# A resampling kernel on one core: the results and the bilinear pass are read from PSUM bank by bank, bank 0 by ScalarE and bank 1 by VectorE

## The chip, the cores and the metric

The kernel runs on one core of one Trainium2 chip. The metric is the device time of one execution in microseconds (us), the median of the runs.

## The reference, cut to what matters

Two layers follow each other on an input of 8 x 512 x 128 x 128 fp32. The first makes a half-size image by a grouped convolution, clusters its channels, fits a mixture to get gates, and adds a gated bilinear enlargement to its input. The second adds a bias, enlarges by 2 with a 12-tap filter along both axes, bends the values (leaky ReLU), and reduces by 2 with the filter again.

```python
def _forward(sx, w_down, w_conv, w_up):
    x = conv(sx, w_down, stride 2, groups)            # 8 x 256 x 64 x 64
    ...                                               # clusters, mixture -> gate
    pre_up = gate[:, :, None, None] * x + x
    up = jnp.repeat(pre_up, 2, axis=1) * w_up[None, :, None, None]
    return _bilinear_up_x2(up) + sx                   # 8 x 512 x 128 x 128

def _L1_conv_ref(input, bias, up_filter, down_filter):
    out = input + bias[None, :, None, None]
    out = _sep_upfirdn(out, up_filter * 2, 2, 1, UP_PAD)     # 256 x 256 a channel
    out = jax.nn.leaky_relu(out, 0.2) * 2.0 ** 0.5
    return _sep_upfirdn(out, down_filter, 1, 2, DOWN_PAD)    # 128 x 128 a channel
```

## The kernel before, in words

The convolutions, clusters and mixture fill the first 1.5 ms. The rest, some 5.9 ms, is `resample()`, and the change lies in it alone. It works on 4096 channel images (8 x 512) in 1024 **units** of four. All filters are matrices that TensorE multiplies with, in quadrants of 64 x 64. A unit goes through these steps, software-pipelined over several slots:

- SP loads the image tile `img` (256 KB), and for every second unit the half-size tile `low` (two loads of 16 rows of channels each).
- The **bilinear pass**: TensorE multiplies `low` with `lin` along the rows (L1217, `b1_acc`, in columns 256 to 383 of banks 0 and 1), ScalarE copies both halves to `low_v` (L1273), and GpSimd (POOL) widens it along the other axis in `widen`, the **lift**: `low_d` (L1050), a small copy (L1051), `low_f` (L1053), `lift` (L1056). POOL also adds the bias to `img` (L1041).
- VectorE makes `x_sum` = lift x coef + img in four instructions of 128 elements (L1315).
- **first_up** (TensorE into banks 0 and 1, `u1_acc`), copied to `up1`, half by ScalarE (L1260), half by VectorE (L1300). **second_up** (banks 2 to 5, `u2_acc`).
- The bend, twice two instructions: ScalarE writes 0.2 of the value to `slope_t` (L1251), VectorE takes the maximum into `leaky` (L1291). "Bend 0" and "bend 1" are the pairs for e = 0 and 1.
- **first_down** (banks 6 and 7, `d1_acc`), copied to `dn` by ScalarE (L1282, `d1_out`). **second_down** (banks 0 and 1, columns 0 to 255, `d2_acc`), whose end raises `d2_mm`; it is called d2 below. ScalarE copies both banks to `res` in one instruction (L1267), and SP stores it.

`twin` is banks 0 and 1 as one tile. In the profile's rows, `twin` and `bank` tell which banks TensorE writes.

Each engine runs its own program of **slots**, one for each unit; semaphores tie them. TensorE's slot is: first_down half 0, second_down half 0, in every second slot the bilinear pass, second_up for e = 1 half 0, second_down half 1, second_up e = 1 half 1, first_down half 1, and then `up_part` of the next unit: first_up half 0, second_up e = 0 half 0, first_up half 1, second_up e = 0 half 1. A slot with the bilinear pass is a **G slot**, one without an **N slot**; two make a pair, and there are 512 pairs. T is the start of first_down half 0. VectorE's slot is: `up1` half, bend 0, x_sum, bend 1. ScalarE's is: `up1` half, slopes for e = 0, res, in G low_v, slopes for e = 1, two dn.

The order between engines around the change: first_down half 0 waits (L1187) until all four `leaky` of the slot before are written and both `dn` of the slot before are copied, since it reads the one and overwrites the source of the other. first_up half 0 waits for x_sum, for res (`res_ready`) and in G slots for low_v (`b1_out`), since it overwrites banks 0 and 1 (L1158, L1160). POOL's lift waits for `b1_out`. SP's store waits for `res_ready`; its next image load waits for an earlier x_sum.

Of the kernel before, what the change touches and what calls it, by code (L numbers as in the profile page):

```python
# [88 lines left out]
def build(nc, x, w_down, w_conv, w_up, bias, up_filter, down_filter, consts, out):  # L89
    at = constants()[1]  # L90
    ctx = ExitStack()
    with ctx:
# [794 lines left out]
        def resample():  # L887
            with ExitStack() as own:
# [22 lines left out]
                res_stored = [sem(f"res_stored{i}") for i in range(2)]  # L911
                biased = sem("biased")
                b1_mm = sem("b1_mm")
                b1_out = sem("b1_out")
                lift_step = sem("lift_step")
                lifted = sem("lifted")
                x_summed = sem("x_summed")
# [10 lines left out]
                d1_out = sem("d1_out")  # L928
                d2_half = sem("d2_half")
                d2_mm = sem("d2_mm")  # L930
                res_ready = sem("res_ready")

# [46 lines left out]
                @block.sync  # L981
                def _(sp):
                    def load_low(u, r, m):

                        g = cnt(u, r, m, 6, per=2)
                        done = cnt(u, r, m, 6, of=2)
                        if u is None:
                            g, done = sp.snap(g), sp.snap(done)
                        if after(u, -4):
                            sp.wait_ge(b1_mm, done)  # L990

                        group = lows[:, bass.ds(g, LOWS), :] if u is None else lows[:, g:g + LOWS, :]
                        sp.dma_start(low[0:HALF], group[:, 0:2]).then_inc(low_loaded, 16)  # L993
                        sp.dma_start(low[HALF:P], group[:, 2:4]).then_inc(low_loaded, 16)  # L994

                    def load_img(u, r, m):

                        p = (m + 1) % 2
                        g = cnt(u, r, m, 3, per=4)
                        used = cnt(u, r, m, 2)  # L1000
                        if u is None:
                            g, used = sp.snap(g), sp.snap(used)
                        if after(u, -1):
                            sp.wait_ge(x_summed, used)
                        sp.dma_start(img[p][:].rearrange("p e i w -> p (e i) w"),
                                     images[:, bass.ds(g, 4), :] if u is None else images[:, g:g + 4, :]).then_inc(img_loaded[p], 16)

                    def store(u, r, m):

                        p = (m - 3) % 2  # L1010
                        g = (u - 3) * 4 if u is not None else sp.snap(r * (4 * STEP) + (m - 3) * 4)
                        sp.wait_ge(res_ready, cnt(u, r, m, -2))
                        sp.dma_start(results[:, bass.ds(g, 4), :] if u is None else results[:, g:g + 4, :], res[p][:]).then_inc(res_stored[p], 16)

                    def slot(u, r, m):
                        if has(u, -3):
                            load_img(u, r, m)
                        if m % 2 == 0 and has(u, -6):
                            load_low(u, r, m)
                        if has(u, 3):  # L1020
                            store(u, r, m)

                    for u in range(-6, FIRST):
                        slot(u, 0, u)
                    schedule(sp, slot)
                    for i in range(2):
                        sp.wait_ge(res_stored[i], 16 * PAIRS // 2)

                @block.gpsimd
                def _(pool):  # L1030
                    pool.wait_ge(small_loaded, 16)
                    weights = const("lin_rest").rearrange("p (w t) -> p w t", t=2)[:, None].to_broadcast([P, LOWS, WO - 1, 2])

                    def add_bias(u, r, m):

                        p = m % 2
                        pool.wait_ge(img_loaded[p], cnt(u, r, m, 2 + 2, per=16, of=2))
                        g = cnt(u, r, m, 2, per=4)
                        bg = bias_all[:, bass.ds(g, 4)] if u is None else bias_all[:, g:g + 4]
                        pix = img[p][:].rearrange("p e i w -> p (e i) w")  # L1040
                        nc.gpsimd.tensor_tensor(pix, pix, bg[:, :, None].to_broadcast([P, 4, W]), ALU.add).then_inc(biased, 1)  # L1041

                    def widen(u, r, m):

                        dst = lift[(m // 2) % 2]
                        if after(u, 0):

                            pool.wait_ge(x_summed, cnt(u, r, m, 2))
                        pool.wait_ge(b1_out, cnt(u, r, m, 6, of=2))
                        nc.gpsimd.tensor_tensor(low_d[:], low_v[:, :, 1:WO], low_v[:, :, 0:WO - 1], ALU.subtract).then_inc(lift_step, 1)  # L1050
                        nc.gpsimd.tensor_copy(dst[:, :, 0:W:W - 1], low_v[:, :, 0:WO:WO - 1]).then_inc(lift_step, 1)  # L1051
                        pool.wait_ge(lift_step, cnt(u, r, m, 4, per=3, of=2) + 1)
                        nc.gpsimd.tensor_tensor(low_f[:], low_d[:, :, :, None].to_broadcast([P, LOWS, WO - 1, 2]), weights,  # L1053
                                                ALU.mult).then_inc(lift_step, 1)
                        pool.wait_ge(lift_step, cnt(u, r, m, 4, per=3, of=2) + 3)
                        nc.gpsimd.tensor_tensor(dst[:, :, 1:W - 1].rearrange("p c (w t) -> p c w t", t=2), low_f[:],  # L1056
                                                low_v[:, :, 0:WO - 1, None].to_broadcast([P, LOWS, WO - 1, 2]), ALU.add).then_inc(lifted, 1)

                    def slot(u, r, m):
                        if has(u, -2):  # L1060
                            add_bias(u, r, m)
                        if m % 2 == 0 and has(u, -4):
                            widen(u, r, m)

                    schedule(pool, slot)

                @block.tensor
                def _(pe):
# [76 lines left out]
                    def up_part(u, r, m):  # L1145
                        p = m % 2
                        if has(u, 0):
                            n_sum = n_of(u, r, m, 1)
                            if after(u, 4):

                                n_res = n_of(u, r, m, -3)
                            if m % 2 == 1:

                                n_b1 = n_of(u, r, m, 5, of=2) if has(u, -3) else PAIRS // 2
                            pe.wait_ge(ready, FILTERS)
                            pe.wait_ge(x_summed, n_sum)
                            if after(u, 4):
                                pe.wait_ge(res_ready, n_res)  # L1158
                            if m % 2 == 1:
                                pe.wait_ge(b1_out, n_b1)  # L1160
                            if u is not None and u < 4:

                                pe.wait_ge(u1_out0, u)
                                pe.wait_ge(u1_out1, u)
                                pe.wait_ge(b1_out, (u + 5) // 2)
                            first_up(p, 0).then_inc(u1_half, 1)
                        if has(u, 1):
                            second_up_begin(u, r, m, 0)
# [7 lines left out]
                    def slot(u, r, m):  # L1176
# [12 lines left out]
                        if has(u, 3):  # L1189
# [6 lines left out]
                            if has(u, 0):  # L1196
                                pe.wait_ge(u1_out0, n_up0)
                                pe.wait_ge(u1_out1, n_up1)
                            else:
                                pe.wait_ge(res_ready, u - 3)  # L1200
                            second_down(1 - p, 0).then_inc(d2_half, 1)
                        if group:

# [4 lines left out]
                            if not has(u, 3):  # L1208

                                if after(u, -2):  # L1210
                                    pe.wait_ge(b1_out, (u + 4) // 2)
                                if has(u, 0):
                                    pe.wait_ge(u1_out0, u + 1)
                                    pe.wait_ge(u1_out1, u + 1)
# [30 lines left out]
                def _(act):  # L1245
# [7 lines left out]
                    def slot(u, r, m):  # L1253
# [9 lines left out]
                        if has(u, 3):  # L1263
                            act.wait_ge(d2_mm, cnt(u, r, m, -2))
                            if after(u, 5):
                                act.wait_ge(res_stored[1 - p], cnt(u, r, m, -3, per=16, of=2))
                            nc.scalar.activation(res[1 - p][:].rearrange("p (e i) w -> p e (i w)", e=2), twin[:, :, 0:D2], ACT.Copy).then_inc(res_ready, 1)  # L1267
                        if m % 2 == 0 and has(u, -4):
                            act.wait_ge(b1_mm, cnt(u, r, m, 6, of=2))
                            if after(u, -2):  # L1270

                                act.wait_ge(lifted, cnt(u, r, m, 4, of=2))
                            nc.scalar.activation(low_v[:].rearrange("p (i c) w -> p i (c w)", i=2), twin[:, :, D2:D2 + 2 * WO], ACT.Copy).then_inc(b1_out, 1)  # L1273
                        if has(u, 1):
                            slope(u, r, m, 1)
                        if has(u, 2):
# [10 lines left out]
                def _(v):  # L1287
# [6 lines left out]
                    def slot(u, r, m):  # L1294
# [6 lines left out]
                        if has(u, 1):  # L1301
                            if after(u, 3):

                                v.wait_ge(d1_mm, cnt(u, r, m, -2))
                            bend(u, r, m, 0)
                        if has(u, -2):

                            n = (m + 2) % STEP
# [48 lines left out]
```

## Time and profile before

| | us |
|---|---|
| median of 3 runs | 7528.47 (7528.38 to 7532.02) |
| the profiled execution | 7524.66 |
| its span | 7522.9 |
| TensorE busy / VectorE / ScalarE / POOL | 7038.6 / 5921.7 / 4569.9 / 2523.5 |
| mean granted TensorE clock | 0.968 of 2.4 GHz |

The profile is one execution. Its rows give for each instruction or group a start from the span's begin, a duration, and where an engine had been idle, what ended that. PE is TensorE's matmul and PEld its weight load; matmul ends are modelled, weight-load starts are not. DVE is VectorE, ACT is ScalarE. A merged row with "x4" runs from the first start to the last end of four instructions.

### The profile page before, as it was taken

What the parts mean: (1) busy time and instruction counts of PE and PEld (TensorE: products, weight loads), DVE (VectorE), ACT (ScalarE), POOL (GpSimd) and SP (SyncE); (2) the same over time, 40 slices, a digit from 0 to 9 for tenths busy, and PEclk for the clock granted to TensorE, in tenths of its full rate; (3) what the DMA queues carried; (4) which work ended last, traced back from release to release, by engine and by line L of the source; (5) the groups of instructions that cost most, each with busy time, mean ns of one, the idle gap of its engine ahead of it and who ended that gap; (6) DMA issues with size and microseconds to landing.
All of it is one profiled execution on the core that took longest, in us unless ns stands there. A gap on an engine that the chain in (4) does not pass through costs nothing.

```text
span 7522.9 us, 691936 instructions
## 1 busy us (share of the span) xinstructions
PE 7038.6 (94%) x302277; PEld 6399.7 (85%) x302277; DVE 5921.7 (79%) x11620; ACT 4569.9 (61%) x9038; POOL 2523.5 (34%) x3076
## 2 busy tenths in 40 slices
PE   6699993089999999999999999999999999999999
PEld 2444441079999999999999999999999999999998
DVE  7399998967777777777777777777777777777776
ACT  0100002357777777777777777777777777777776
POOL 0000000034444444444444444444444444444443
PEclk9799996589999999999999999999999999999999
DMA  6188883023333333333333333333333333333332
GB/s 259 59 321 316 324 316 111 0 78 95 97 96 95 98 95 96 96 95 97 96 95 98 95 96 97 95 96 96 95 97 95 96 97 95 97 96 95 97 95 82
DMA packets 1261249, 891.87 MB, mean 119 GB/s; under 512 B 184336, under 2 KB 1234960, under 8 KB 1244432
## 3 DMA queue, kind: packets, MB, share of 16 engines
q1 hardware_dynamic: 1249936, 856.58, 36.9%
q10 hardware_dynamic: 11264, 34.61, 1.6%
q8 instruction: 34, 0.56, 0.0%
q14 instruction: 15, 0.12, 0.0%
HBM read 587.94 MB, written 303.04 MB: 118 GB/s over the span
## 4 chain that ended last, share of the span: by engine, by line
PE 79%; issue 0%; DVE 0%; DMA 0%; ACT 0%; SPq 0%; POOL 0%; DVEq 0%
PE bank L1087 26%; PE bank L1082 25%; PE twin L1082 13%; PE twin L1087 13%; PE twin L1217 2%; DVE x_sum L1315 0%; DMA img<-in_x 0%; DVE leaky L1291 0%; DMA low<-conv_dram 0%; SPq L993 0%; POOL img L1041 0%; SPq L994 0%; DVE up L1300 0%; ACT dn L1282 0%; ACT res L1267 0%
## 5 line engine op out<-in xcount | busy, mean ns | idle before, releaser
L1291 DVE SCALAR_TENSOR_TENSOR leaky<-bank,slope_t 128x512 f32<-128x512 f32 x4096 | 2634.4, 684 | 1036.8 <-ACT slope_t L1251 1036.8
L1082 PE MATMUL bank<-up_t,up 64*64 64x133 f32 x65536 | 2761.8, 276 | 2.0 <-issue 1.2
L1087 PEld LDWEIGHTS bank<-down_t,leaky 64*64 64x64 f32 x131072 | 2241.0, 135 | 101.5 <-issue 92.6
L1087 PE MATMUL bank<-down_t,leaky 64*64 64x35 f32 (+1 forms) x131072 | 2312.1, 222 | 13.5 <-issue 11.6
L1251 ACT ACTIVATE slope_t<-bank 128x512 f32<-128x512 f32 x4096 | 2226.2, 600 | 2.7 <-PE bank L1082 2.7
L1082 PEld LDWEIGHTS bank<-up_t,up 64*64 64x64 f32 x65536 | 2044.6, 134 | 3.3 <-issue 3.3
L1050 POOL TENSOR_TENSOR low_d<-low_v 128x252 f32<-128x252 f32 x512 | 311.2, 608 | 4901.9 <-ACT low_v L1273 4901.9
L1267 ACT ACTIVATE res<-twin 128x512 f32<-128x512 f32 x1024 | 611.5, 597 | 1452.9 <-PE twin L1087 1452.9
L1315 DVE SCALAR_TENSOR_TENSOR x_sum<-lift,coef,img 128x128 f32<-128x128 f32 x4096 | 1432.5, 409 | 11.8 <-POOL img L1041 11.8
L1082 PE MATMUL twin<-up_t,x_sum 64*64 64x133 f32 x32768 | 1385.9, 278 | 7.5 <-DVE x_sum L1315 5.3
L1087 PE MATMUL twin<-down_t,dn 64*64 64x35 f32 (+1 forms) x65536 | 1359.7, 222 | 7.1 <-issue 6.7
L1087 PEld LDWEIGHTS twin<-down_t,dn 64*64 64x64 f32 x65536 | 1263.3, 135 | 8.0 <-issue 7.9
L1282 ACT ACTIVATE dn<-bank 128x512 f32<-128x512 f32 x2048 | 1137.5, 628 | 7.5 <-PE bank L1087 7.5
L1041 POOL TENSOR_TENSOR img<-img,bias_all 128x512 f32<-128x512 f32 x1024 | 1044.4, 1042 | 7.9 <-DMA img<-in_x 7.7
L1082 PEld LDWEIGHTS twin<-up_t,x_sum 64*64 64x64 f32 x32768 | 1007.0, 133 | 8.9 <-issue 8.8
L1300 DVE COPY up<-twin 128x512 f32<-128x512 f32 x1024 | 708.0, 691 | 291.2 <-PE twin L1082 269.9
L361 PE MATMUL twin<-rows_next,diag 128*128 128x448 f32 (+1 forms) x2016 | 809.6, 559 | 16.9 <-DMA rows_next<-in_x 16.3
L332 DVE SCALAR_TENSOR_TENSOR conv_next<-rows_next,tap_w,conv_next 128x576 f32<-128x576 f32 (+3 forms) x952 | 770.8, 810 | 33.7
L361 PEld LDWEIGHTS twin<-rows_next,diag 128*128 128x128 f32 x2016 | 375.2, 188 | 433.9 <-issue 399.8
L1260 ACT ACTIVATE up<-twin 128x512 f32<-128x512 f32 x1024 | 611.4, 597 | 122.2 <-PE twin L1082 75.3
L1056 POOL TENSOR_TENSOR lift<-low_f,low_v 128x504 f32<-128x504 f32 x512 | 568.8, 1111 | 40.2
L1053 POOL TENSOR_TENSOR low_f<-low_d,cst 128x504 f32<-128x504 f32 x512 | 571.3, 1116 | 0.0
(159 smaller groups left out, 1788.0 us busy)
## 6 DMA issues: line engine op xcount, KB each, us to landing
img<-in_x SPq DMA_DIRECT2D x1024, 256.0 KB, 2.9
out<-res SPq DMA_DIRECT2D x1024, 256.0 KB, 2.4
rows_next<-in_x SPq DMA_DIRECT2D x42, 4224.0 KB, 13.9
rows_next<-in_x SPq DMA_DIRECT2D x14, 4096.0 KB, 13.5
low<-conv_dram SPq DMA_DIRECT2D x1024, 32.0 KB, 2.2
conv_dram<-conv_next ACTq DMA_DIRECT2D x56, 512.0 KB, 4.1
rows_in<-in_x SPq DMA_DIRECT2D x6, 4224.0 KB, 14.0
rows_in<-in_x SPq DMA_DIRECT2D x2, 4096.0 KB, 29.1
```

The costliest lines, as they stand in the source:

```text
L332: ins = v.scalar_tensor_tensor(out=dst, in0=src, scalar=w, in1=dst, op0=ALU.mult, op1=ALU.add)
L361: mm = pe.matmul(acc[:, :, (1 if kw == 0 else 0):], diag[:, cb * TAPS + (i * 3 + kh) * 3 + kw, :], conv_in(rows_in, n, i, kh, kw, V_ROWS, ...
L1041: nc.gpsimd.tensor_tensor(pix, pix, bg[:, :, None].to_broadcast([P, 4, W]), ALU.add).then_inc(biased, 1)
L1082: return pe.matmul(acc[cols(c), a:b], src[cols(rt), cols(c)], up_t[cols(rt), a:b], start=first, stop=False, skip_group_check=True)
L1087: return pe.matmul(acc[cols(c), a:b], src[cols(rt)], down_t[cols(rt), k, a:b], start=first, stop=False, skip_group_check=True)
L1251: nc.scalar.activation(slope_t[e][i][:], u2_acc[e][i][:], ACT.Copy, scale=SLOPE * GAIN).then_inc(slope_out, 1)
L1260: nc.scalar.activation(up1[p][:, 0].rearrange("p e h -> p (e h)"), u1_acc[0], ACT.Copy).then_inc(u1_out0, 1)
L1267: nc.scalar.activation(res[1 - p][:].rearrange("p (e i) w -> p e (i w)", e=2), twin[:, :, 0:D2], ACT.Copy).then_inc(res_ready, 1)
L1282: nc.scalar.activation(dn1[p][:, e].rearrange("p j i h -> p (j i h)"), d1_acc[e][:], ACT.Copy).then_inc(d1_out, 1)
L1291: v.scalar_tensor_tensor(out=leaky[1 - m % 2][:, e, i].rearrange("p k w -> p (k w)"), in0=u2_acc[e][i][:], scalar=GAIN, in1=slope_t[e][i][ ...
L1300: v.tensor_copy(up1[m % 2][:, 1].rearrange("p e h -> p (e h)"), u1_acc[1]).then_inc(u1_out1, 1)
L1315: ins = v.scalar_tensor_tensor(out=x_sum[n % 2][:, e, i, :], in0=lift[n // 2][:, 2 * (n % 2) + e, :], scalar=cf, in1=img[n % 2][:, e, i, : ...
```

## The change

ScalarE's instruction for `res` and its instruction for `low_v` are each cut to bank 0 (half the elements). VectorE copies the half in bank 1, both right after bend 0 and ahead of its four x_sum. `res_ready` and `b1_out` become two semaphores each, one for each bank, and who waited for one waits for both: SP's store, POOL's lift, TensorE's first_up, and the places of the pipeline's start and end.

```diff
-                b1_out = sem("b1_out")
+                b1_out = [sem(f"b1_out{e}") for e in range(2)]
...
-                res_ready = sem("res_ready")
+                res_ready = [sem(f"res_ready{e}") for e in range(2)]
...
-                        sp.wait_ge(res_ready, cnt(u, r, m, -2))
+                        for e in range(2):
+                            sp.wait_ge(res_ready[e], cnt(u, r, m, -2))
...
-                        pool.wait_ge(b1_out, cnt(u, r, m, 6, of=2))
+                        for e in range(2):
+                            pool.wait_ge(b1_out[e], cnt(u, r, m, 6, of=2))
...
                             if after(u, 4):
-                                pe.wait_ge(res_ready, n_res)
+                                pe.wait_ge(res_ready[0], n_res)
+                                pe.wait_ge(res_ready[1], n_res)
                             if m % 2 == 1:
-                                pe.wait_ge(b1_out, n_b1)
+                                pe.wait_ge(b1_out[0], n_b1)
+                                pe.wait_ge(b1_out[1], n_b1)
...
-                            nc.scalar.activation(res[1 - p][:].rearrange("p (e i) w -> p e (i w)", e=2), twin[:, :, 0:D2], ACT.Copy).then_inc(res_ready, 1)
+                            nc.scalar.activation(res[1 - p][:, 0:2].rearrange("p i w -> p (i w)"), d2_acc[0][:, 0:D2], ACT.Copy).then_inc(res_ready[0], 1)
...
-                            nc.scalar.activation(low_v[:].rearrange("p (i c) w -> p i (c w)", i=2), twin[:, :, D2:D2 + 2 * WO], ACT.Copy).then_inc(b1_out, 1)
+                            nc.scalar.activation(low_v[:, 0:2].rearrange("p c w -> p (c w)"), b1_acc[0], ACT.Copy).then_inc(b1_out[0], 1)
...
                             bend(u, r, m, 0)
+                        if has(u, 3):
+
+                            v.wait_ge(d2_mm, cnt(u, r, m, -2))
+                            if after(u, 5):
+                                v.wait_ge(res_stored[1 - m % 2], cnt(u, r, m, -3, per=16, of=2))
+                            v.tensor_copy(res[1 - m % 2][:, 2:4].rearrange("p i w -> p (i w)"), d2_acc[1][:, 0:D2]).then_inc(res_ready[1], 1)
+                        if m % 2 == 0 and has(u, -4):
+                            v.wait_ge(b1_mm, cnt(u, r, m, 6, of=2))
+                            if after(u, -2):
+
+                                v.wait_ge(lifted, cnt(u, r, m, 4, of=2))
+                            v.tensor_copy(low_v[:, 2:4].rearrange("p c w -> p (c w)"), b1_acc[1]).then_inc(b1_out[1], 1)
```

## Rows read from the trace of the kernel before

**Rows 1.** The page's part 1: busy us, share, instructions.

```profile
PE 7038.6 (94%) x302277; PEld 6399.7 (85%) x302277; DVE 5921.7 (79%) x11620; ACT 4569.9 (61%) x9038; POOL 2523.5 (34%) x3076
```

**Rows 2.** Timeline, weight loads: start us, us, what, count.

```profile
5002.39 1.11 PEld L1087 LDWEIGHTS bank<-down_t,leaky 64*64 64x64 f32 x64
...
5005.17 1.11 PEld L1087 LDWEIGHTS bank<-down_t,leaky 64*64 64x64 f32 x64
5006.15 0.47 PEld L1082 LDWEIGHTS twin<-up_t,x_sum 64*64 64x64 f32 x16
...
5008.14 1.07 PEld L1087 LDWEIGHTS bank<-down_t,leaky 64*64 64x64 f32 x64 [0.15 <-issue]
...
5011.16 1.11 PEld L1087 LDWEIGHTS bank<-down_t,leaky 64*64 64x64 f32 x64
5012.23 0.46 PEld L1082 LDWEIGHTS twin<-up_t,x_sum 64*64 64x64 f32 x16
...
5014.09 1.05 PEld L1087 LDWEIGHTS bank<-down_t,leaky 64*64 64x64 f32 x64
...
5019.77 1.05 PEld L1087 LDWEIGHTS bank<-down_t,leaky 64*64 64x64 f32 x64 [0.15 <-issue]
```

**Rows 3.** Timeline, POOL, three pairs.

```profile
5012.09 0.61 POOL L1050 TENSOR_TENSOR low_d<-low_v 128x252 f32<-128x252 f32 x1 [6.70 <-ACT low_v L1273]
...
5012.80 1.11 POOL L1053 TENSOR_TENSOR low_f<-low_d,cst 128x504 f32<-128x504 f32 x1
...
5035.33 0.61 POOL L1050 TENSOR_TENSOR low_d<-low_v 128x252 f32<-128x252 f32 x1 [6.69 <-ACT low_v L1273]
```

**Rows 4.** Timeline, ScalarE, an N slot and a G slot.

```profile
5005.07 0.60 ACT L1267 ACTIVATE res<-twin 128x512 f32<-128x512 f32 x1 [1.13 <-PE twin L1087]
...
5011.14 0.60 ACT L1267 ACTIVATE res<-twin 128x512 f32<-128x512 f32 x1 [1.65 <-PE twin L1087]
5011.64 0.38 ACT L1273 ACTIVATE low_v<-twin 128x256 f32<-128x256 f32 x1
...
5012.85 1.12 ACT L1282 ACTIVATE dn<-bank 128x512 f32<-128x512 f32 x2
```

**Rows 5.** Timeline, VectorE, the same G slot.

```profile
5010.24 1.13 DVE L1315 SCALAR_TENSOR_TENSOR x_sum<-lift,coef,img 128x128 f32<-128x128 f32 x4
5012.54 1.29 DVE L1291 SCALAR_TENSOR_TENSOR leaky<-bank,slope_t 128x512 f32<-128x512 f32 x2 [1.16 <-ACT slope_t L1251]
```

**Rows 6.** Groups of VectorE's instructions, whole span, shapes apart: busy us, mean ns, idle.

```profile
L1315 DVE SCALAR_TENSOR_TENSOR x_sum<-lift,coef,img 128x128 f32<-128x128 f32 x4096 | 1432.5, 409 | 11.8 <-POOL img L1041 11.8
L1300 DVE COPY up<-twin 128x512 f32<-128x512 f32 x1024 | 708.0, 691 | 291.2 <-PE twin L1082 269.9
...
L808 DVE COPY tot<-bank 128x34 f32<-128x34 f32 x10 | 1.9, 194 | 7.3 <-PE bank L859 7.3
```

**Rows 7.** Timeline in the stage's ramp, x_sum against POOL's lift.

```profile
1529.65 3.15 DVE L1315 SCALAR_TENSOR_TENSOR x_sum<-lift,coef,img 128x128 f32<-128x128 f32 x4 [10.17 <-POOL img L1041]
```

**Rows 8.** Timeline in the ramp, the next meeting of the two.

```profile
1547.29 0.96 DVE L1315 SCALAR_TENSOR_TENSOR x_sum<-lift,coef,img 128x128 f32<-128x128 f32 x2
1547.43 0.67 POOL L1050 TENSOR_TENSOR low_d<-low_v 128x252 f32<-128x252 f32 x1 [4.73 <-ACT low_v L1273]
...
1548.17 0.34 DVE L1315 SCALAR_TENSOR_TENSOR x_sum<-lift,coef,img 128x128 f32<-128x128 f32 x1
...
1548.27 1.21 POOL L1053 TENSOR_TENSOR low_f<-low_d,cst 128x504 f32<-128x504 f32 x1
```

**Rows 9.** The tile img in 100 us: duration ns min/median/max, DMA landing.

```profile
L1041 POOL TENSOR_TENSOR img<-img,bias_all x18: 1032/1040/1045, 5003.4 to 5097.3; 128x512 f32<-128x512 f32 x18
...
DMA to landing us min/median/max: 2.8/2.9/3.2
```

**Rows 10.** Stretches of the ramp: busy us of each engine, granted clock, DMA share.

```profile
1570.00:1580.00 10.00, 8.18 (x312) 7.96 (x307) 4.32 (x9) 4.39 (x8) 2.56 (x3) 0.83 0.27 73
1580.00:1590.00 10.00, 10.00 (x531) 9.83 (x522) 7.42 (x15) 6.96 (x14) 4.92 (x6) 1.00 0.24 65
```

More of the change, by code:

```diff
@@ L1164, in up_part @@
                                 pe.wait_ge(u1_out1, u)
-                                pe.wait_ge(b1_out, (u + 5) // 2)
+                                pe.wait_ge(b1_out[0], (u + 5) // 2)
+                                pe.wait_ge(b1_out[1], (u + 5) // 2)
                             first_up(p, 0).then_inc(u1_half, 1)
@@ L1199, in slot @@
                             else:
-                                pe.wait_ge(res_ready, u - 3)
+                                pe.wait_ge(res_ready[0], u - 3)
+                                pe.wait_ge(res_ready[1], u - 3)
                             second_down(1 - p, 0).then_inc(d2_half, 1)
@@ L1210, in slot @@
                                 if after(u, -2):
-                                    pe.wait_ge(b1_out, (u + 4) // 2)
+                                    pe.wait_ge(b1_out[0], (u + 4) // 2)
+                                    pe.wait_ge(b1_out[1], (u + 4) // 2)
                                 if has(u, 0):
```

## The prediction

> **What bounds the kernel now.** I read four things in this order.
>
> First the page's busy shares: TensorE is at 94% of the whole span, VectorE at 79% [rows 1]. That says "TensorE-bound", but an end of a matmul is modelled in this profile, so a short stall between two groups of matmuls doesn't show as idle time. So I went to the starts of TensorE's weight loads, in order of time.
>
> Second, those starts [rows 2]. Call T the start of first_down's first half, with which a slot of TensorE begins. N slots (no bilinear pass) last 5008.14 - 5002.39 = 5.75 us and 5019.77 - 5014.09 = 5.68, 5.71 on average; the G slot (bilinear pass) 5014.09 - 5008.14 = 5.95. The lift's first instruction comes once a pair and gives the mean: (5035.33 - 5012.09) / 2 = 11.62 us a pair [rows 3], so G is 5.91 on average. That is the number to change; there are 512 pairs.
>
> Third, what ends slot G. ScalarE starts `res` at 5011.14 (T + 3.00) and then works without a pause: res, low_v, two slopes, two dn, the last ending at 5012.85 + 1.12 = 5013.97 [rows 4]. TensorE's next T is 5014.09, 0.12 later [rows 2]; it waits for both `d1_out`. So in this slot TensorE touches ScalarE's chain. In slot N `res` starts at T + 2.68 (5005.07) and nothing like this binds.
>
> Fourth, VectorE in the same slot [rows 5]: the four x_sum end at 5011.37, VectorE then waits for a slope until 5012.54, and the second pair of `leaky` (bend 1) ends at 5013.83. TensorE's next slot needs all four `leaky`, so it can't begin before that. Between d2's end (5011.14) and T (5014.09) there are 2.95 us, and today VectorE has only 1.29 us of needed work in them. The change puts more there.
>
> **The change part by part.**
>
> *ScalarE loses two halves.* `res` falls from 512 elements (0.60 us) to 256, and low_v of 256 took 0.38 [rows 4, 6], so res saves 0.22. For low_v from 256 to 128 I take half of that, 0.11. ScalarE's chain in slot G becomes 0.33 shorter, and its hold on T there goes. By itself that is worth at most the stall it ended. The other slots G, where nothing is held, can't be shorter than 11.62 x 2 - 5.75 - 5.95 - 5.68 = 5.86: 0.09 in half of the pairs.
>
> *VectorE gains two copies, at the place where d2 ends.* No row shows a 256- or 128-element copy from PSUM by VectorE. The same copy at 512 takes 0.691 and at 34, in an earlier stage, 0.194 [rows 6]: 1.04 ns an element, so 0.42 for res (256) and 0.29 for b1 (128). The bounds are half of 0.691, 0.35, and 0.69. A following instruction starts 0.08 before the end of the one ahead (two `leaky` of 0.68 and 0.69 take 1.29 together) [rows 5]. The Trainium skill ("VectorE: DVE Perf Modes", the TRN2 errata's cycle table) gives a VectorE read of PSUM (120 + elements) cycles at 0.96 GHz: 0.66 us for 512, where the row has 0.69; an estimate by that page would be 0.39 and 0.26, and slot G 0.06 shorter than below.
>
> *x_sum moves behind these copies, into POOL's work.* This is the costly part. Today x_sum in G runs from 5010.24 to 5011.37 while POOL rests; POOL starts low_d 0.07 after low_v ends [rows 3, 4, 5]. In the new order VectorE's b1 copy is the last thing POOL waits for, and x_sum is the next instruction on VectorE. So both start together. What that does stands in the ramp of this stage: at 1529.65 four x_sum over POOL's lift took 3.15 us in place of 1.13 [rows 5, 7]. The arrangement at 1547 is the one the new slot G will have [rows 8]: an x_sum starts at 1547.29, low_d 0.14 after it and 0.67 long, the next x_sum is held until low_d is over: the two end together at 1547.29 + 0.96 = 1548.25, 0.15 after low_d. The one that starts at 1548.17 takes 0.34, then low_f starts at 1548.27 and runs to 1549.48. There VectorE had no fourth x_sum left. In the new slot it has: it starts behind low_f's start and, held in the same way, ends 0.15 after low_f, at 1549.63 on that clock, so 2.20 after low_d's start. The `leaky` instructions are not held: 0.68 to 0.69 beside low_f (5012.80 to 5013.91) [rows 3, 5]. The Trainium skill ("SBUF — State Buffer", SBUF: two separate sides) says that a VectorE instruction with two SBUF inputs and a GpSimd instruction take a shared port pair exclusively, one blocking the other for its whole length; by that rule x_sum (two SBUF inputs) is held and leaky (one of PSUM) is not, and the trace agrees in both.
>
> *Slot G from T.* d2 ends for VectorE at +2.96 (3.00 in [rows 2, 4]; slots G differ by 0.09, so I take 2.96). From there: res ends +0.42; b1 starts +0.34 and ends +0.63; POOL's low_d starts +0.71; the fourth x_sum ends 0.71 + 2.20 = +2.91; bend 1 starts 0.08 before that, +2.83, and ends +4.12; TensorE follows after the 0.12 of ScalarE's release, +4.24. Slot G = 2.96 + 4.24 = 7.20 us, against 5.91.
>
> *Slot N from T.* d2 at +2.69; x_sum starts +0.34 and takes 1.13 if POOL is done; bend 1 ends at +0.34 + 1.13 - 0.08 + 1.29 = +2.68, TensorE +0.12: 5.49. That is under the 5.71 of TensorE's own work, so VectorE is covered there by 0.22. POOL is done if its two image additions are (1.04 us each [rows 9]): the first needs nothing, the second an image whose load waits for slot G's x_sum (T + 2.96 + 2.91 = 5.87), and which lands 2.9 after its issue begins [rows 9]. With 0.4 for SP to get to it that is T + 9.2; the addition runs to about 10.2, and slot N's x_sum starts at 7.20 + 2.69 + 0.34 = 10.23. They touch. It costs nothing as long as the delay is under 0.22.
>
> *One more wait on TensorE ahead of first_up.* Today the boundary from first_down's second half to first_up is 0.98 us in N and 1.07 in G [rows 2]; G has one wait more there (x_sum, res and low_v, against x_sum and res), and I put the 0.09 down to it. The change takes N from two waits to three and G from three to five, and I take 0.09 for N, which becomes 5.80. In G what they cost lies under VectorE's 7.20. Bounds: 0 and 0.18. SP's store and POOL's lift get a second wait as well, behind which only the image load and the lift are queued; the first semaphore is up earlier than before, so they wait for VectorE's alone, which is up at d2 + 0.63 where ScalarE's low_v ended at 5012.02, d2 + 0.88 [rows 4].
>
> Sum: a pair takes 5.80 + 7.20 = 13.00 us instead of 11.62, +1.38. Over 508 pairs (512 less the ramps at both ends) it is +701 us. On the profiled execution's 7524.7 us that makes 8226; the median of the runs lies 3.8 higher, so 8230. The stages ahead of this one aren't touched.
>
> **The rivals.**
>
> *x_sum is not held up in G* (POOL and VectorE interleave better than at 1547). Then x_sum takes 1.13: bend 1 ends at 0.55 + 1.13 - 0.08 + 1.29 = +2.89, slot G = 2.96 + 2.89 + 0.12 = 5.97, about what TensorE needs with its added wait. A pair is 11.8 and the time about 7620. Against it stand all rows in which the two meet, x_sum's mean of 409 ns among them [rows 6, 7, 8]. Held up by one POOL instruction instead of two (x_sum 1.6 to 1.9), slot G is 6.45 to 6.75 and the time 7850 to 8000.
>
> *Slot N is hit as well*: the second image addition begins before x_sum in N and holds its first instruction to the end, up to +0.85. N then becomes up to 6.3, and the time up to 8480.
>
> *TensorE's clock falls.* New gaps of 1.3 us come once a pair. In the ramp, 10 us with TensorE busy for 8.18 ran at a granted clock of 0.83, and the next 10 at 1.00 [rows 10], so the clock does fall in this stage when TensorE waits often enough. If a tenth of the stage ran at 1.2 GHz, TensorE's work of 11.6 a pair would add 1.16, some 590 us. [...]
>
> *Faster: ScalarE's chain is what holds T and VectorE has room.* For it speaks that VectorE idles from 5011.37 to 5012.54 in G [rows 5]. G would fall by the 0.09 above in half of the pairs: about -23 us, 7505. It decides only if x_sum and both copies end by the time the slopes are ready, 1.39 after d2 less the 0.33 that ScalarE gains, so 1.06. They end at 1.60 at best. I see no way.
>
> *The change does nothing to the time*: the same condition, with the added wait eating the gain.
>
> **Chances.** Forecast (8120 to 8400) 0.70, partly held (7800 to 8120) 0.10, not held (7600 to 7800) 0.06, slot N hit or the clock down (above 8400) 0.07, faster 0.04, same 0.03. The range 7800 to 8450 holds the first two and the low end of the fourth, 0.83; its upper bound also takes the copies at 0.69 (+0.27 and up to +0.1 in G, about 190 us). Within 0.2%, 15 us, this kernel can't be told from no change. Faster 0.04, same 0.03, slower 0.93.
>
> **What would show it.** TensorE's T to T is 7.2 and 5.8 in turn. ScalarE's res takes 0.38, VectorE's 0.42 and 0.29. In G the first x_sum starts 0.15 ahead of low_d, x_sum's mean in the stage rises from 409 to above 480 ns, and four of them take 2.3 us; in N 1.13. VectorE has no idle time between its copies and bend 1. TensorE's wait for leaky appears in the list of waits, 1.3 us or a bit less, 512 times. I would be wrong if x_sum in G took 1.13, or if T to T of G stayed under 6.2.

## The result and the profile after

The changed kernel takes 8248.86 us, the kernel before 7530.25 on the same chip: a ratio of 1.095 (95% interval 1.094 to 1.0966). The forecast was 8230. Over 508 pairs the difference of 718.6 us is 1.41 us a pair.

TensorE's weight loads, in order of time, as in [rows 2] (start us, us):

```profile
5006.16 1.05 PEld L1089 LDWEIGHTS bank<-down_t,leaky 64*64 64x64 f32 x64 [1.05 <-issue]
...
5008.87 1.11 PEld L1089 LDWEIGHTS bank<-down_t,leaky 64*64 64x64 f32 x64
5009.94 0.46 PEld L1084 LDWEIGHTS twin<-up_t,x_sum 64*64 64x64 f32 x16
...
5011.93 1.26 PEld L1089 LDWEIGHTS bank<-down_t,leaky 64*64 64x64 f32 x64 [0.16 <-issue]
5013.08 0.59 PEld L1089 LDWEIGHTS twin<-down_t,dn 64*64 64x64 f32 x32
...
5019.25 1.05 PEld L1089 LDWEIGHTS bank<-down_t,leaky 64*64 64x64 f32 x64 [1.15 <-issue]
...
5025.02 1.26 PEld L1089 LDWEIGHTS bank<-down_t,leaky 64*64 64x64 f32 x64 [0.16 <-issue]
```

Slot N is 5011.93 - 5006.16 = 5.77 us and 5025.02 - 5019.25 = 5.77. Slot G is 5019.25 - 5011.93 = 7.32, and the next one 7.23 (T at 5032.25). Before, they were 5.71 and 5.91. So the loss is in G: about +1.36, and +0.06 in N. Ahead of the T that follows a G slot the loads now pause for 1.05 to 1.15 us; there was no such pause before. In the list of waits (5000 to 5500 us: in total, times, longest) they stand so, together with the short pauses behind the branch of TensorE's loop:

```profile
PEld bank L1089 <- issue: 48.0, 76, 1.2
```

VectorE in the same G slot and the N slot after it, as in [rows 5]:

```profile
5015.07 0.42 DVE L1318 COPY res<-twin 128x256 f32<-128x256 f32 x1 [0.96 <-PE twin L1089]
5015.41 0.28 DVE L1324 COPY low_v<-twin 128x128 f32<-128x128 f32 x1
5015.63 2.36 DVE L1334 SCALAR_TENSOR_TENSOR x_sum<-lift,coef,img 128x128 f32<-128x128 f32 x4
5017.91 1.27 DVE L1298 SCALAR_TENSOR_TENSOR leaky<-bank,slope_t 128x512 f32<-128x512 f32 x2
...
5021.95 0.42 DVE L1318 COPY res<-twin 128x256 f32<-128x256 f32 x1 [0.98 <-PE twin L1089]
5022.30 1.13 DVE L1334 SCALAR_TENSOR_TENSOR x_sum<-lift,coef,img 128x128 f32<-128x128 f32 x4
```

VectorE has no idle time from d2 (5015.07) to the end of bend 1 (17.91 + 1.27 = 5019.18), and TensorE's T is 0.07 later. Four x_sum take 2.36 us in G and 1.13 in N. POOL beside them, as in [rows 3]:

```profile
5015.84 0.61 POOL L1052 TENSOR_TENSOR low_d<-low_v 128x252 f32<-128x252 f32 x1 [6.78 <-DVE low_v L1324]
5016.39 0.27 POOL L1053 COPY lift<-low_v 128x8 f32<-128x8 f32 x1
5016.62 1.22 POOL L1055 TENSOR_TENSOR low_f<-low_d,cst 128x504 f32<-128x504 f32 x1
5017.92 1.11 POOL L1058 TENSOR_TENSOR lift<-low_f,low_v 128x504 f32<-128x504 f32 x1
5018.98 1.04 POOL L1042 TENSOR_TENSOR img<-img,bias_all 128x512 f32<-128x512 f32 x1
5021.06 1.04 POOL L1042 TENSOR_TENSOR img<-img,bias_all 128x512 f32<-128x512 f32 x1 [1.03 <-DMA img<-in_x]
```

The first x_sum starts 0.21 ahead of low_d, the fourth ends at 5017.99, 0.15 after low_f (5017.84). The second image addition now waits for its DMA and ends at 5022.10, 0.20 ahead of slot N's x_sum.

From the page's groups (busy us, mean ns, idle before), as in [rows 6]:

```profile
L1334 DVE SCALAR_TENSOR_TENSOR x_sum<-lift,coef,img 128x128 f32<-128x128 f32 x4096 | 1789.4, 497 | 2.7 <-POOL img L1042 2.5
L1274 ACT ACTIVATE res<-twin 128x256 f32<-128x256 f32 x1024 | 393.5, 384 | 2077.3 <-PE twin L1089 2077.3
L1318 DVE COPY res<-twin 128x256 f32<-128x256 f32 x1024 | 434.2, 424 | 974.7 <-PE twin L1089 974.7
```

### The profile page after: what moved, and what is told of

Its sections match the earlier page's. It is cut to its first block, busy times and chain, and to the rows that moved or that the text cites. A ratio compares the mean times of both kernels' runs of the same rounds, so it can differ in the third digit from the quotient of the medians.

```text
span 8247.8 us, 697567 instructions
## 1 busy us (share of the span) xinstructions
PE 7312.2 (89%) x302277; PEld 6507.7 (79%) x302277; DVE 6673.0 (81%) x13156; ACT 4386.7 (53%) x9038; POOL 2627.4 (32%) x3076
## 4 chain that ended last, share of the span: by engine, by line
PE 76%; issue 6%; DVE 0%; POOL 0%; DMA 0%; ACT 0%; SPq 0%; POOLq 0%; DVEq 0%
PE bank L1089 27%; PE bank L1084 23%; PE twin L1084 13%; PE twin L1089 12%; PE twin L1224 2%; DVE x_sum L1334 0%; DVE leaky L1298 0%; DMA low<-conv_dram 0%; POOL lift L1058 0%; POOL low_f L1055 0%; POOL img L1042 0%; DVE up L1307 0%; SPq L993 0%; ACT dn L1289 0%; POOL low_d L1052 0%
## 5 line engine op out<-in xcount | busy, mean ns | idle before, releaser
L1089 PEld LDWEIGHTS bank<-down_t,leaky 64*64 64x64 f32 x131072 | 2312.9, 135 | 672.4 <-issue 659.0
L1089 PE MATMUL bank<-down_t,leaky 64*64 64x35 f32 (+1 forms) x131072 | 2417.4, 222 | 462.4 <-issue 460.1
L1334 DVE SCALAR_TENSOR_TENSOR x_sum<-lift,coef,img 128x128 f32<-128x128 f32 x4096 | 1789.4, 497 | 2.7 <-POOL img L1042 2.5
L1274 ACT ACTIVATE res<-twin 128x256 f32<-128x256 f32 x1024 | 393.5, 384 | 2077.3 <-PE twin L1089 2077.3
L1042 POOL TENSOR_TENSOR img<-img,bias_all 128x512 f32<-128x512 f32 x1024 | 1064.1, 1039 | 573.3 <-DMA img<-in_x 573.3
L1318 DVE COPY res<-twin 128x256 f32<-128x256 f32 x1024 | 434.2, 424 | 974.7 <-PE twin L1089 974.7
L1289 ACT ACTIVATE dn<-bank 128x512 f32<-128x512 f32 x2048 | 1120.3, 610 | 10.0 <-PE bank L1089 10.0
L1055 POOL TENSOR_TENSOR low_f<-low_d,cst 128x504 f32<-128x504 f32 x512 | 623.2, 1217 | 0.0
```

What stands on the lines that cost most here:

```text
L1089: return pe.matmul(acc[cols(c), a:b], src[cols(rt)], down_t[cols(rt), k, a:b], start=first, stop=False, skip_group_check=True)
L1289: nc.scalar.activation(dn1[p][:, e].rearrange("p j i h -> p (j i h)"), d1_acc[e][:], ACT.Copy).then_inc(d1_out, 1)
L1334: ins = v.scalar_tensor_tensor(out=x_sum[n % 2][:, e, i, :], in0=lift[n // 2][:, 2 * (n % 2) + e, :], scalar=cf, in1=img[n % 2][:, e, i, : ...
```

## The experiments

Theory A is that of the forecast: x_sum, put behind the copies, is late and begins together with POOL's lift, which holds it. Rival B: VectorE's added copies cost what they take. Rival C: TensorE's added waits.

### lift_waits: the order kept, the meeting taken away

```diff
-                        if after(u, 0):
+                        if after(u, -2):
-                            pool.wait_ge(x_summed, cnt(u, r, m, 2))
+                            pool.wait_ge(x_summed, cnt(u, r, m, 3))
```

> The changed kernel; POOL's lift in slot G also waits for the x_sum of the same slot, so that it begins only when VectorE is through with them; the order on VectorE stays. Theory A (half of the loss and more is the collision of x_sum with the lift): four x_sum take 1.13 in place of 2.36, slot G falls from 7.3 to about 6.1, the time to 7620 to 7700. Rival B (the late start alone, or the copies): G stays at 7.2, above 8150. Rival C (the added waits on TensorE): no change either.

7795.83 us, 1.0347 of before (1.0326 to 1.0369). Weight loads, then VectorE (N slot, G slot), then POOL:

```profile
5001.94 1.11 PEld L1089 LDWEIGHTS bank<-down_t,leaky 64*64 64x64 f32 x64
...
5008.12 1.16 PEld L1089 LDWEIGHTS bank<-down_t,leaky 64*64 64x64 f32 x64 [0.52 <-issue]
...
5014.12 1.11 PEld L1089 LDWEIGHTS bank<-down_t,leaky 64*64 64x64 f32 x64
```

```profile
5005.06 1.78 DVE L1334 SCALAR_TENSOR_TENSOR x_sum<-lift,coef,img 128x128 f32<-128x128 f32 x4
5006.77 1.27 DVE L1298 SCALAR_TENSOR_TENSOR leaky<-bank,slope_t 128x512 f32<-128x512 f32 x2
...
5011.61 1.13 DVE L1334 SCALAR_TENSOR_TENSOR x_sum<-lift,coef,img 128x128 f32<-128x128 f32 x4
```

```profile
5003.88 2.04 POOL L1042 TENSOR_TENSOR img<-img,bias_all 128x512 f32<-128x512 f32 x2
5013.05 0.61 POOL L1052 TENSOR_TENSOR low_d<-low_v 128x252 f32<-128x252 f32 x1 [7.14 <-DVE x_sum L1334]
```

In G x_sum is back to 1.13 and the slot to 6.00 (5014.12 - 5008.12): the meeting alone was worth 7.27 - 6.00 = 1.27 us a pair, with both copies and all the waits in place. The time misses the expected 7700 because POOL is now later: its two image additions (5003.88 to 5005.92) run into slot N's x_sum, which takes 1.78, and N rises to 6.18 (5008.12 - 5001.94) and 6.14. The collision had moved, and some 0.38 us of the gain went with it.

It had moved to where it stood in the kernel before. There POOL's image additions met x_sum in N slots, which is what raised its mean to 409 ns:

```profile
5003.36 2.04 POOL L1041 TENSOR_TENSOR img<-img,bias_all 128x512 f32<-128x512 f32 x2
5004.76 1.57 DVE L1315 SCALAR_TENSOR_TENSOR x_sum<-lift,coef,img 128x128 f32<-128x128 f32 x4
5006.26 1.29 DVE L1291 SCALAR_TENSOR_TENSOR leaky<-bank,slope_t 128x512 f32<-128x512 f32 x2
```

Before, bend 1 ended at 5007.55, 0.59 ahead of T (5008.14), and the meeting was free. With the res copy ahead of x_sum it ends at 5008.04 in lift_waits, and T is 0.08 later.

### b1_only and res_only: one copy at a time

In both, the copy that VectorE no longer makes goes back to ScalarE, and whoever waited for its two halves waits for one semaphore. The diffs show the main lines.

b1_only: VectorE copies only its half of low_v, behind ScalarE's res.

```diff
+   nc.scalar.activation(res[1 - p][:]..., twin[:, :, 0:D2], ACT.Copy).then_inc(res_ready[0], 1)   # both banks
...
                             v.wait_ge(b1_mm, cnt(u, r, m, 6, of=2))
+                            if has(u, 3):
+                                v.wait_ge(res_ready[0], cnt(u, r, m, -2))
                             v.tensor_copy(low_v[:, 2:4]..., b1_acc[1]).then_inc(b1_out[1], 1)
```

> The changed kernel, but res is copied by ScalarE alone as before; VectorE copies only its half of low_v (0.28 us, once a pair), ahead of its x_sum and behind ScalarE's res. Theory A (what counts is that x_sum starts together with POOL's lift): x_sum starts at d2 + 0.87, 0.14 ahead of low_d, takes 2.3 to 2.4, slot G is 7.4 to 7.5 and N 5.75: 8330 to 8400 us, slower than the changed kernel with less than a third of its added work. Rival B (the copies' own time, 0.28 a pair): under 7700.

8419.99 us, 1.1182 (1.1166 to 1.1198), a little above what was expected: slots G take 7.58 to 7.78 us and not 7.4 to 7.5. VectorE and POOL in a G slot:

```profile
5012.43 0.29 DVE L1318 COPY low_v<-twin 128x128 f32<-128x128 f32 x1 [1.58 <-issue]
5012.66 2.35 DVE L1328 SCALAR_TENSOR_TENSOR x_sum<-lift,coef,img 128x128 f32<-128x128 f32 x4
5014.94 1.27 DVE L1296 SCALAR_TENSOR_TENSOR leaky<-bank,slope_t 128x512 f32<-128x512 f32 x2
```

```profile
5012.86 0.62 POOL L1052 TENSOR_TENSOR low_d<-low_v 128x252 f32<-128x252 f32 x1 [6.97 <-DVE low_v L1318]
```

res_only: VectorE copies its half of res, ScalarE both halves of low_v.

```diff
                             act.wait_ge(b1_mm, cnt(u, r, m, 6, of=2))
+                            if has(u, 3):
+                                act.wait_ge(res_ready[1], cnt(u, r, m, -2))
...
+   nc.scalar.activation(low_v[:]..., twin[:, :, D2:D2 + 2 * WO], ACT.Copy).then_inc(b1_out[0], 1)   # both banks
-   v.tensor_copy(low_v[:, 2:4]..., b1_acc[1]).then_inc(b1_out[1], 1)
```

> The changed kernel, but low_v is copied by ScalarE alone, which first waits for VectorE's res (both read bank 1); VectorE copies res only, ahead of x_sum. ScalarE's low_v ends at about d2 + 0.9, so POOL's low_d starts when VectorE has three of its four x_sum behind it. Theory A: only the last x_sum is held, by low_d: four take 1.4 to 1.6 in place of 2.36, slot G 6.15 to 6.35, N 5.77 to 5.8, the time 7650 to 7770 us. Rival B (the copies' own time, 0.42 a slot against 0.28 a pair in b1_only): slower than b1_only's 8420 or near the changed kernel's 8249.

7651.24 us, 1.0161 (1.0147 to 1.0176). VectorE and POOL in a G slot:

```profile
5009.70 0.42 DVE L1317 COPY res<-twin 128x256 f32<-128x256 f32 x1 [0.92 <-PE twin L1089]
5010.04 1.48 DVE L1327 SCALAR_TENSOR_TENSOR x_sum<-lift,coef,img 128x128 f32<-128x128 f32 x4
```

```profile
5010.75 0.62 POOL L1052 TENSOR_TENSOR low_d<-low_v 128x252 f32<-128x252 f32 x1 [6.89 <-ACT low_v L1279]
```

This pair decides against rival B. b1_only adds 0.28 us of VectorE work a pair and loses 890 us; res_only adds 0.42 a slot, 0.84 a pair, and loses 119. Two things differ. One is where low_d starts: 0.20 after the first x_sum in the one, 0.71 after it in the other, when only the fourth is left to be held (1.48 in all, against 2.35). The other is where x_sum itself starts: 0.92 after d2 in b1_only, whose copy waits for ScalarE's res, and 0.35 in res_only. Of the 1.58 us between their mean slots G (7.68 and 6.10) the first makes 0.87 and the second 0.57.

### before_sums_late: x_sum late without any copy

```diff
+                            if m % 2 == 0 and has(u, -4):
+                                v.wait_ge(b1_out, cnt(u, r, m, 6, of=2))
                             v.wait_ge(lifted, cnt(u, r, m, 2 + 2, of=2))
```

> The kernel before, with one wait more on VectorE in slot G: its x_sum wait for ScalarE's low_v. No copy moves to VectorE, TensorE's waits are as before. Theory A: x_sum starts at d2 + 0.93 together with POOL's lift and takes 2.3, bend 1 ends at d2 + 4.4, slot G is 7.4 to 7.5, the time 8280 to 8350, as slow as the changed kernel without any of its copies. If x_sum were late but not held (1.13), G would be 6.3 and the time 7730. Rival B (the copies' time is the cost): under 7600.

9114.37 us, 1.2098 (1.2073 to 1.2122): the direction of A and far more than A said. VectorE and POOL:

```profile
5012.35 3.17 DVE L1317 SCALAR_TENSOR_TENSOR x_sum<-lift,coef,img 128x128 f32<-128x128 f32 x4 [1.97 <-ACT low_v L1273]
```

```profile
5012.19 0.61 POOL L1050 TENSOR_TENSOR low_d<-low_v 128x252 f32<-128x252 f32 x1 [8.35 <-ACT low_v L1273]
...
5014.27 1.10 POOL L1056 TENSOR_TENSOR lift<-low_f,low_v 128x504 f32<-128x504 f32 x1
```

Two things were missing in the expectation. Here POOL starts 0.16 ahead of VectorE, so each of the four x_sum meets one of POOL's four instructions and the last waits for `lift` too: 3.17, where [rows 7] have 3.15 and the changed kernel, with x_sum 0.21 ahead, has 2.36. So who is first by 0.2 us is worth 0.8. x_sum also starts 1.11 after d2 (5011.24) and not 0.93, and slot G is 8.56 (5016.79 - 5008.23) in place of 7.4 to 7.5. And TensorE's pauses grew to about 2.6 us, and its clock began to fall. Stretches (busy us of PE, PEld, DVE, ACT, POOL, then the granted clock):

```profile
5000.00:5003.00 3.00, 2.04 (x108) 2.07 (x112) 3.00 (x7) 0.00 (x0) 0.76 (x2) 0.90 0.32 87
5003.00:5006.00 3.00, 3.00 (x104) 3.00 (x99) 1.52 (x3) 1.21 (x3) 0.84 (x1) 0.53 0.00 0
5006.00:5010.00 4.00, 4.00 (x200) 3.84 (x196) 2.89 (x5) 3.17 (x6) 0.00 (x0) 1.00 0.48 131
```

A pause of 2.63 us ended at 5000.93. From 5002.4 to 5005.8 the clock stood at the lower level (1.2 GHz) and the slot N took 7.30 us (5008.23 - 5000.93); after the pause that ended at 5016.79, 2.55 long, it did not fall and N took 5.68. The length of the pause doesn't tell the two cases apart: in the steady part of the stage the clock fell after 158 of 492 such pauses, every third or fourth, and lengths from 2.51 to 2.64 stand on both sides. What picks them isn't shown. The falls cost 158 x 1.62, some 256 us of the 764 by which the time lies above the expected 8350. The changed kernel, whose pauses are 1.05 to 1.15, has a granted clock of 1.00 from 1600 to 8200 us (0.971 over the whole execution, the stages ahead of this one included), so this rival had no part in it.

### sums_from_psum: the same meeting, with one input in PSUM

In the loop x_sum reads 128 columns of bank 1 in place of lift, so that term of the output is left out, and first_up waits for that reading.

```diff
-                            n_sum = n_of(u, r, m, 1)
+                            n_sum = n_of(u, r, m, 2 if u is None else 1)
-   in0=lift[n // 2][:, 2 * (n % 2) + e, :],
+   in0=lift[n // 2][:, 2 * (n % 2) + e, :] if u is not None else d2_acc[1][:, 0:W],
```

> The changed kernel; in the loop x_sum takes 128 columns of bank 1 in PSUM in place of lift (so the output is wrong in that term), and TensorE waits for that reading ahead of first_up. Theory A in its narrow form (VectorE is held because x_sum has two inputs in SBUF): four x_sum take 1.1 to 1.2 us beside POOL's lift; bend 1 then ends in time, first_up is held by x_sum's end instead, G about 6.4, N about 6.2, the time 7900 to 8050. Rival D (any VectorE instruction with a scalar read from SBUF, or of this length, is held): x_sum stays at 2.3 and G at 7.3 or more, above 8250.

8138.08 us, 1.0807 (1.0791 to 1.0823). VectorE and POOL in a G slot, then the groups of 500 us:

```profile
5008.99 1.13 DVE L1334 SCALAR_TENSOR_TENSOR x_sum<-twin,coef,img 128x128 f32<-128x128 f32 x4
```

```profile
5009.21 0.61 POOL L1052 TENSOR_TENSOR low_d<-low_v 128x252 f32<-128x252 f32 x1 [7.59 <-DVE low_v L1324]
```

```profile
L1334 DVE SCALAR_TENSOR_TENSOR x_sum<-twin,coef,img 128x128 f32<-128x128 f32 x312 | 87.3, 343 | 0.0
L1084 PE MATMUL twin<-up_t,x_sum 64*64 64x133 f32 x2496 | 105.1, 279 | 29.6 <-DVE x_sum L1334 19.0 <-issue 10.6
```

The first x_sum starts 0.22 ahead of low_d, as in the changed kernel, and four take 1.13 in place of 2.36; the scalar from SBUF and the other input from SBUF are still there. So it is the second tensor input from SBUF that gets it held. No run gives x_sum another second SBUF input than lift, so that it is their number and not this tile is in part argued: POOL writes the other buffer of lift at that time, and `leaky`, with one SBUF input, takes 1.27 beside POOL's lift as elsewhere (5017.91 in the changed kernel). The time is above the 7900 to 8050 expected, as first_up now waits for x_sum in both slots (6.2 to 6.3 in N, 6.5 to 6.65 in G). The Trainium skill ("SBUF — State Buffer", SBUF: two separate sides) says the shared ports are locked against a VectorE instruction with two SBUF inputs for the whole length of the GpSimd one. This run agrees, set beside the changed kernel: 343 ns for the mean x_sum against 497.

### before_pe_waits: TensorE's added waits alone

```diff
                                 pe.wait_ge(res_ready, n_res)
+                                pe.wait_ge(taps_loaded, 16)
                             if m % 2 == 1:
                                 pe.wait_ge(b1_out, n_b1)
+                                pe.wait_ge(small_loaded, 16)
```

> The kernel before, with TensorE's added waits alone: ahead of first_up one more wait in every slot and one more in slots G, both on semaphores of the loads at the start, which have long been up. The forecast's term: 0.09 us in N and about 0.1 in G, so 7600 to 7630 us. Rival C2: the waits ride along with others and cost nothing, 7530.

These are as many as the change adds: one in N and two in G, three a pair. 7629.29 us, 1.0126 (1.0105 to 1.0147): +99 us, 0.195 us a pair, as the forecast's 0.09 and 0.1. The boundary from first_down's second half to first_up grows from 0.98 to 1.07 in N and from 1.07 to 1.17 in G. Waits on semaphores that are long up are not free for a TensorE that never pauses. In the changed kernel G's part lies under VectorE's 7.3 us; N grows by 0.06.

### sums_first, sums_first_one_sem, g_slots_only: what the change could have brought

sums_first: the two copies stand behind the four x_sum on VectorE.

```diff
                         if has(u, -2):
                             ...                       # the four x_sum
+                        if has(u, 3):
+                            ...                       # res, bank 1
+                        if m % 2 == 0 and has(u, -4):
+                            ...                       # low_v, bank 1
                         if has(u, 1):
                             bend(u, r, m, 1)
```

> The changed kernel with VectorE's two copies moved behind its four x_sum. Theory A (the loss is x_sum standing behind the copies, where it is late and meets POOL's lift): x_sum in G is back to 1.13 us ahead of the lift, bend 1 ends at about T + 5.0, so TensorE sets both slots, N 5.77, G about 5.9 to 6.0: 7530 to 7600 us. Rival B (it is VectorE's added work of 0.7 us in G, wherever it stands): G stays above 6.5 and the time above 7850.

7864.12 us, 1.0438 (1.0416 to 1.0459). In G x_sum is 1.13 again and the slot 6.10, but the time misses the expectation, at a value that rival B had named. Slot N, weight loads and VectorE:

```profile
5005.10 1.11 PEld L1089 LDWEIGHTS bank<-down_t,leaky 64*64 64x64 f32 x64
...
5009.27 0.46 PEld L1084 LDWEIGHTS twin<-up_t,x_sum 64*64 64x64 f32 x16 [0.28 <-issue]
```

```profile
5007.47 1.36 DVE L1322 SCALAR_TENSOR_TENSOR x_sum<-lift,coef,img 128x128 f32<-128x128 f32 x4
5008.74 0.41 DVE L1330 COPY res<-twin 128x256 f32<-128x256 f32 x1
```

In N d2 ends at 5007.77 by ScalarE, but VectorE is in x_sum until 5008.83 (1.36 and not 1.13, as POOL's image additions run to 5007.89), its res copy ends at 5009.15, and first_up starts at 5009.27 in place of about 5008.86 (0.98 after 5007.88). I had looked at bend 1 alone and not at who waits for res.

sums_first_one_sem counts both halves on one semaphore, with as many waits as before:

```diff
-    pe.wait_ge(res_ready[0], n_res); pe.wait_ge(res_ready[1], n_res)
+    pe.wait_ge(res_ready, n_res)        # n_res = n_of(u, r, m, -3, per=2); b1_out likewise
```

> The kernel sums_first with one semaphore for both engines' halves, counted twice, so that TensorE, POOL and SP have as many waits as in the kernel before. Theory A with the waits' term: G falls from 6.10 to about 5.90; N stays near 6.15, since first_up is held there by VectorE's late res copy and not by the number of waits: 7720 to 7770 us. Rival C (the waits are what is left of the loss): 7560 or less.

7822.82 us, 1.0389 (1.0374 to 1.0404), above the expected 7720 to 7770 and far from rival C's 7560. G fell by 0.15 to 5.96, N rose to 6.2 to 6.3: first_up still waits for res there. The waits were 41 us of the 334 and not the rest.

g_slots_only leaves N's res to ScalarE alone:

```diff
+                            if m % 2 == 0:
                                 nc.scalar.activation(...d2_acc[0]...).then_inc(res_ready, 1)
+                            else:
+                                nc.scalar.activation(...twin[:, :, 0:D2]...).then_inc(res_ready, 2)
-                        if has(u, 3):
+                        if m % 2 == 0 and has(u, 3):           # VectorE's res
```

> sums_first_one_sem, and in N slots res is copied by ScalarE alone. Nothing is late then: x_sum is ahead of d2 in both slots, ScalarE's chain in G is 0.33 shorter, no wait is added. Theory A: N 5.71, G 5.86 to 5.90, the time 7500 to 7530 us, so what the change could have brought at the most. If VectorE's copies cost something by themselves it is above 7545.

> The same kernel as g_slots_only once more, on whichever chip comes, since its runs stood at two levels (two at 7513 and 7517, nine at 7571 to 7574). If the levels belong to the kernel they show again; if to the chip or the session, all runs stand together. By the slots of its trace (5.74 and 5.85 us) it should take 7510 to 7520.

Both series, on two chips, stand at the same two levels: 7513.34, 7517.44 and 7517.67 us, and nineteen runs from 7570.50 to 7577.64. So the levels go with the execution and not with the chip. (Of the kernel before, single runs at 7556.65 and 7558.89 stand out in two of the sessions; the others lie from 7523 to 7537.) The ratios of the medians are 1.0049 (1.0036 to 1.0062) and 1.0047 (1.0032 to 1.0063): no gain. The upper level is above the 7545 from which the copies were to cost something by themselves, the lower one is where no cost was expected; so that question stays open, at 0.5% or less. One profile fell on each level. Weight loads of the lower one (7513.34):

```profile
5003.20 1.07 PEld L1087 LDWEIGHTS bank<-down_t,leaky 64*64 64x64 f32 x64 [0.15 <-issue]
5004.22 0.59 PEld L1087 LDWEIGHTS twin<-down_t,dn 64*64 64x64 f32 x32
```

and of the upper one (7574.55):

```profile
5004.01 1.15 PEld L1087 LDWEIGHTS bank<-down_t,leaky 64*64 64x64 f32 x64 [0.16 <-issue]
5005.12 0.59 PEld L1087 LDWEIGHTS twin<-down_t,dn 64*64 64x64 f32 x32
```

The same instructions, in the slot that follows the branch of TensorE's loop, take 1.02 us to the next group in the one and 1.11 in the other. Slot G is 5.85 (5009.05 - 5003.20) against 5.96 (5009.97 - 5004.01), and 0.11 x 508 is 56 us, most of the 61 between the two profiled executions.

## Why the prediction was right

- **Where the bound is**: right. T of the slot after G hung on ScalarE's chain by little; now it hangs on bend 1 (0.07 after its end). In the list of waits it stands as "issue" and not as leaky, against what I had said would show.
- **Slot G**: forecast 2.96 + 4.24 = 7.20, measured 7.32 and 7.23. From d2 (5015.07) on: low_d +0.77 for +0.71, the fourth x_sum +2.92 for +2.91, bend 1's end +4.11 for +4.12, T +4.18 for +4.24. The copies are 0.424 and 0.28 for 0.42 and 0.29. The term that was mis-sized is the 2.96 ahead of d2, measured 3.13 (5015.06 by ScalarE, less 5011.93) and about 3.05 in the next G slot: first_down half 0 takes 1.15 behind the loop's branch (5011.93 to 5013.08) where it was 1.03 before (5008.14 to 5009.17). The two levels of g_slots_only are a part of the same stretch. Why isn't shown.
- **The meeting with POOL**: right, and shown by lift_waits (1.27 us a pair), res_only against b1_only, and sums_from_psum.
- **Slot N**: forecast 5.80, measured 5.77. The image addition ended 0.20 ahead of x_sum, so that rival stayed out; lift_waits shows it real, at 1.78 for x_sum. The forecast took 1.13 for x_sum in N without saying that it took 1.57 to 1.80 there before: by coming later, x_sum got clear of the image additions.
- **The added waits**: the boundary ahead of first_up in N grew by 0.09 as forecast (5009.94 - 5008.87 = 1.07, for 0.98). The slot grew by 0.06 only, as first_down half 0 takes 0.93 behind the new pause (5006.16 to 5007.09), where it took 0.96 on average. Alone the waits are 0.195 a pair.
- **The rival on the other side**: what its premise, ScalarE's shorter chain, can give is in g_slots_only's G of 5.85, against 5.91. It doesn't show in the median.
- **The upper bound of the range**: its working adds up to 0.1 for the second copy in G at 0.69, where 0.69 less 0.29 would be 0.40. The copies took 0.424 and 0.28, so the slip had no effect.
- **TensorE's clock**: it didn't fall, with a granted clock of 1.00 through the stage.

Sum: 13.00 forecast, 5.77 + 7.27 = 13.04 measured, and 8230 against 8248.86.

## What to carry to other kernels

A free stretch on an engine is worth nothing without its place: what stands behind the new work moves too, and here it moved into another engine's work on the same ports. Look for the instruction that releases the neighbour and for the one that follows it on the same engine; if they start together, take the price from the place in the trace where the two once met. Before moving a copy, list every waiter of it in each kind of slot: sums_first mended slot G and was then held in slot N by the waiter of res.

## What was not expected of the hardware

- Who starts first decides how many instructions are held: x_sum 0.2 us ahead of the lift takes 2.36 for four, 0.16 behind it 3.17, and 0.7 ahead of it 1.48, against 1.13 alone.
- TensorE's clock fell to 1.2 GHz after 158 of 492 pauses of 2.51 to 2.64 us in before_sums_late, and their length doesn't tell which. It never fell after the changed kernel's pauses of 1.05 to 1.16.
- The same program ran at two levels 0.8% apart, and the difference is 0.1 us in one group of weight loads behind a loop's branch. What sets it is open.
- Three waits more a pair, on semaphores long up, cost TensorE 0.195 us a pair.
